# Moving layer 0's step products from GpSimd to VectorE, and layer 1's output projection behind the next image's first states

## The chip, the cores and the metric

The kernel runs on one core of a Trainium2 chip. A core has five engines that run their own instruction streams and meet at semaphores: TensorE (PE, matrix products into PSUM), VectorE (DVE), ScalarE (ACT), GpSimd (POOL) and SyncE (SP, which issues the DMAs here). The metric is the device time of one execution in microseconds (us), lower is better. PSUM is the memory into which TensorE writes (`bank` in the code), SBUF the larger one beside it (`room`, `u`, `y`, `pictures` and the rest).

## What is computed

Eight images of 32x32 pixels and 192 channels run through two layers. Cut to what matters, with `_gn` a group norm and `L` = 1024 pixels:

```python
def layer0(x):                        # 384 inner channels, 16 states, 8 scan orders
    xc, z = split(_gn(x) @ W_in.T)    # then a 3x3 depthwise convolution and silu on xc
    for k in range(8):                # rows, columns, mirrored, and each of them backwards
        dts, B, C = split(x_proj[k] @ xs[k])
        delta = softplus(dt_proj[k] @ dts + bias[k])
        h = exp(delta * A) * h + (delta * xs[k]) * B      # a scan over the 1024 pixels, per state
        y[k] = sum_n(h[n] * C[n]) + D[k] * xs[k]
    return layernorm(sum_k y[k]) * silu(z) @ W_out.T
def layer1(x):                        # the same frame, four orders with one set of weights,
    ...                               # and decay * cumsum(source / decay) in place of the scan
    return layernorm(y) * silu(z) @ W_out
x = x + layer0(x); x = x + layer1(x)
```

## The kernel before

The images are worked through one after the other; for each, layer 0's scans, layer 0's tail, layer 1's front, layer 1's scans and layer 1's tail. The tail of layer 1 also holds the front of the next image's layer 0 (input projection, convolution, first projections). Every engine has its whole order written out by hand, as a function per stage (`scans0`, `tail0`, `front1`, `scans1`, `tail1`); an engine takes its own instructions strictly in that order, and semaphores tie the orders together.

Layer 0's scans run over 384 units per image: `UNITS` counts g over 8 scan orders i, 3 channel tiles j of 128 channels and 16 states n. The 16 units of one (i, j) are called a pass here, so an image has 24 passes. Tiles are 128 partitions x 1024 pixels in float32. For one unit:

- POOL multiplies the pass's step product `du0` (delta times the input, one tile per pass, two buffers) with a row of B that a DMA has spread over the partitions: `source` (L1186). It may run up to 5 units ahead of the scans (`SOURCES`), and waits then for `scan(g - 5)`.
- ACT makes exp(delta * A) into PSUM: `decay` (L930), two buffers, waiting for `scan(g - 2)`.
- DVE does the scan (`scan`, L1355), decay from PSUM and source from SBUF.
- The state is weighted with C and summed over n by PE, in one of three ways. For 9 of 16 states ("by vector") PE spreads the row of C into two PSUM banks called `WORK` (`spread_c`, L584) and DVE multiplies (`weigh`, L1363). For 3 to 5 states ("by pool": n of 2, 6, 10, for tile 0 also 12, sometimes 8) POOL multiplies with a spread row, three units behind its own sources (`POOL_LAG`, L1195). The others ("by turn": 4, 8, 14, and 12 for tiles 1 and 2) PE transposes into `WORK` (L605), ACT scales (L949).

DVE's order is scan 0, scan 1, weighing 0, scan 2, weighing 1 and so on: the weighing of unit g - 1 behind the scan of unit g. `WORK` is the only room for the spread rows, for the turned states and for the "pieces" (projections for coming passes, L454, L556, L566), so each of these waits until the one before has been taken out.

The step product of the next pass is made by POOL behind its source 6 (`du`, L1176), as two instructions of 512 elements per partition: even lines of pixels, and odd lines backwards. For passes 0 to 11 lines are rows of the picture; for passes 12 to 23 they are columns, and `u` is read with a stride. The first pass's product stands at the head of `scans0`.

Layer 1's output projection (`tail1`, L792) is 12 matrix products (24 matmuls in the trace) of two halves c of the output channels by three tiles j by two halves of pixels. It stands on PE behind `head0` of the next image, that is, behind the first projections, and ahead of the first `spread_c`; its first half goes to the banks `YACC`, its second to `WORK`. ACT takes both out (`take_out1`, L1093) in its units 1 and 2, DVE adds them to the image (`residual`, L1495) behind scan 3 into `pictures`. Scan 4 waits for that, since the buffer `o2` lies in the states' room.

Of the kernel before, what the change touches and what calls it, by code (L numbers as in the profile page):

```python
# [6 lines left out]
ALU = mybir.AluOpType  # L7
# [27 lines left out]
LAST_SUM, FIRST_TERM = 2, 4  # L35

# [120 lines left out]

def mm(step):

    return "mm0" if step in AHEAD else "mm"  # L160


def ev(step):

    return "ev0" if step in AHEAD else "ev"
# [20 lines left out]
def program(nc, counts, images, x, out, w_in, conv_w, conv_b, w_x0, w_dt0, dt_b0, a_log0, d0,  # L186
# [3 lines left out]
    with ctx:  # L190
# [77 lines left out]
        o2 = room[0:CH, 18:20, :]  # L268
# [3 lines left out]
        def whole(lo):  # L272
# [10 lines left out]
                 "xz", "shift", "silu", "mm", "ev", "mm0", "ev0", "stat0", "stat1", "gs0", "gs1", "xn", "pad", "conv", "u",  # L283
                 "p1", "p2", "parts", "dl", "du",
# [25 lines left out]
        def _(sp):  # L310
# [51 lines left out]
            def rows0(b):  # L362
                store_bc(b, 0, 0)
                for g, (i, j, n) in enumerate(UNITS):
# [6 lines left out]
                    if by_pool(i, j, n):  # L371
                        c = POOLED.index((i, j, n))
                        if c == CROWS - 1 and b > 0:

                            sp.wait_ge(S["mm"], at("mm", ("out", 1, 1), b - 1))
# [63 lines left out]
        def _(pe):  # L439
# [170 lines left out]
            def begin_sums(b, i, j):  # L610
                if i * J + j > 0:
                    pe.wait_ge(S["y_turned"], at("y_turned", i * J + j - 1, b))
                elif b > 0:
                    pe.wait_ge(S["ev"], at("ev", ("out", 1, 0), b - 1))
# [46 lines left out]
            def scans0(b):  # L661
                for g in range(len(UNITS) + LAST_SUM + 1):
# [22 lines left out]
                    if n == FIRST_TERM:  # L685
                        begin_sums(b, i, j)
# [67 lines left out]

            def tail1(b):
# [29 lines left out]
                pe.wait_ge(S["load_wout1"], at("load_wout1", 0, b))  # L785
                for c, banks in ((0, (YACC, YACC + 1)), (1, WORK)):
                    if c == 1:
                        wait_free(0, 1)
                    for j in range(J):
                        pe.wait_ge(S["gat"], at("gat", (1, j), b))  # L790
                        for h in range(2):
                            ins = nc.tensor.matmul(bank[0:CH, banks[h], :], wout[1][:, j, c * CH:(c + 1) * CH],  # L792
                                                   y[:, j, halves(h)], start=(j == 0), stop=(j == J - 1))
                    ins.then_inc(S["mm"], note("mm", ("out", 1, c)))
                free[0] = free[1] = ("ev", ("out", 1, 1), b)
# [15 lines left out]
        def _(act):  # L811
# [157 lines left out]
            def scans0(b):  # L969
                for g in range(len(UNITS) + 2):  # L970
# [8 lines left out]
                    if g in (1, 2) and b > 0:  # L979
                        take_out1(b - 1, g - 1)  # L980
# [110 lines left out]
            def take_pair(b, step, dst, banks, rows=P, func=ACT.Copy, **kw):  # L1091
                act.wait_ge(S["mm"], at("mm", step, b))
                nc.scalar.activation(dst, bank[0:rows, banks[0]:banks[1] + 1, :].rearrange("p h t -> p (h t)"),  # L1093
                                     func, **kw).then_inc(S["ev"], note("ev", step))
# [20 lines left out]
            def take_out1(b, c):  # L1115
                take_pair(b, ("out", 1, c), o2[:, c, :], ((YACC, YACC + 1), WORK)[c], rows=CH)

            def tail0(b):
# [4 lines left out]
                for c, banks in ((0, WORK), (1, SPARE)):  # L1123
                    take_pair(b, ("out", 0, c), o2[:, c, :], banks, rows=CH)
# [41 lines left out]
        def _(pool):  # L1166
            def du(b, l, i, j):
                if l == 1:
                    pool.wait_ge(S["dl"], at("dl", (1, 0, j), b))
                    pool.wait_ge(S["yinit"], at("yinit", (1, j), b))  # L1170
                    nc.gpsimd.tensor_tensor(u[:, j, :], delta1[:, j, :], u[:, j, :], ALU.mult).then_inc(
                        S["du"], note("du", (1, 0, j)))
                    return
                pool.wait_ge(S["dl"], at("dl", (0, i, j), b))
                for d, dt, src in zip(stored(du0[:, (i * J + j) % 2, :]), stored(delta0[:, j, :]), lines(u[:, j, :], SCANS[i][1])):
                    nc.gpsimd.tensor_tensor(d, dt, src, ALU.mult).then_inc(S["du"], note("du", (0, i, j)))  # L1176
# [21 lines left out]
            def scans0(b):  # L1198
                du(b, 0, 0, 0)
                for g in range(len(UNITS)):  # L1200
                    source(b, g)
                    i, j, n = UNITS[g]
                    if g >= POOL_LAG and by_pool(*UNITS[g - POOL_LAG]):
                        weigh(b, g - POOL_LAG)
                    ahead = i * J + j + 1
                    if n == 6 and ahead < PASSES:
# [413 lines left out]
```

## Time and profile before

| | us |
|---|---|
| median of 3 runs (15345.07 to 15356.31) | 15351.98 |
| the profiled execution, its own time | 15355.73 |
| its span, first to last instruction | 15353.9 |
| DVE busy in the span (91%) | 13974.8 |
| POOL busy (89%) | 13679.9 |
| PE busy (78%) | 11962.6 |
| ACT busy (67%) | 10343.2 |

All eight images look alike. Of some 1912 us for one, layer 0's scans take 1183, layer 0's tail and layer 1's front some 100, layer 1's scans some 566 and the tail of layer 1 the rest. In a timeline a row is a start, a duration, engine, line, operation, what it writes and reads, and how many like instructions were drawn together; in brackets is the idle time of the engine before it and what ended that. Instructions of an engine overlap by some 0.06 to 0.09 us, so starts lie a little closer than durations say.

### The profile page before, as it was taken

The page shows a single profiled execution, that of the slowest core. Times are in us where ns is not written, and L with a number is a line of the kernel's source. Part 1 is how long each engine was busy: PE and PEld are TensorE (multiplying, and loading weights), DVE is VectorE, ACT ScalarE, POOL GpSimd, SP SyncE. Part 2 cuts the span into 40 slices and gives each one's busy share as a digit, 9 for nine tenths or more (in the row PEclk, how much of TensorE's full clock was granted, in tenths as well). Part 3 has the DMA queues.
Part 4 walks back from the last instruction along what each step waited for, and adds up shares of the span by engine and source line. Part 5 has one row for each costly group of instructions (what it writes and reads, how often), then busy time and mean ns, then how long its engine had stood idle before and what let it go on. Part 6 is the DMA issues. An engine that isn't in the chain of part 4 may idle for free.

```text
span 15353.9 us, 137291 instructions
## 1 busy us (share of the span) xinstructions
PE 11962.6 (78%) x45056; PEld 6538.9 (43%) x45056; DVE 13974.8 (91%) x8019; ACT 10343.2 (67%) x14003; POOL 13679.9 (89%) x5828
## 2 busy tenths in 40 slices
PE   6777877778777787777877778777787777877778
PEld 4543345433444334443345433444334443345433
DVE  8998989989899899998999989999898998989988
ACT  5666766667666676666766667666676666766667
POOL 7997989979899798997889978899789997899978
PEclk8898988989889898898988989889898898988989
DMA  5662256622566225662256622666226662266622
GB/s 188 213 214 95 88 188 215 213 93 85 193 214 215 90 82 196 215 215 86 82 201 213 216 85 80 204 215 214 84 77 209 215 214 81 77 212 214 213 76 76
DMA packets 687758, 2440.08 MB, mean 159 GB/s; under 512 B 78268, under 2 KB 100040, under 8 KB 687048
## 3 DMA queue, kind: packets, MB, share of 16 engines
q1 hardware_dynamic: 687048, 2431.29, 46.6%
q8 instruction: 362, 5.93, 0.2%
q14 instruction: 348, 2.85, 0.1%
HBM read 2415.26 MB, written 15.73 MB: 158 GB/s over the span
## 4 chain that ended last, share of the span: by engine, by line
POOL 48%; issue 18%; DMA 11%; DVE 10%; PE 10%; ACT 3%; POOLq 0%; DVEq 0%; SPq 0%; ACTq 0%
POOL room L1186 26%; DMA room<-bc_rows 11%; POOL room L1229 7%; POOL room L1195 4%; POOL room L1232 4%; POOL room L1221 4%; DVE room L1420 4%; PE bank L720 3%; POOL room L1176 2%; PE bank L454 2%; DVE room L1355 2%; DVE u L1312 1%; DVE room L1440 1%; DVE room L1429 1%; PE bank L792 1%
## 5 line engine op out<-in xcount | busy, mean ns | idle before, releaser
L1355 DVE TENSOR_TENSOR_SCAN room<-bank,room 128x1024 f32<-128x1024 f32 x3072 | 6903.6, 2275 | 327.5 <-issue 170.2
L1186 POOL TENSOR_TENSOR room<-room 128x1024 f32<-128x1024 f32 x3072 | 7168.0, 2374 | 0.6
L930 ACT ACTIVATE bank<-room,a 128x1024 f32<-128x1024 f32 x3072 | 3429.7, 1127 | 1046.0 <-DVE room L1355 1031.7
L720 PE MATMUL bank<-room,identity 128*128 128x512 f32 x6144 | 3007.4, 640 | 855.5 <-DVE room L1440 733.2
L1420 DVE TENSOR_TENSOR_SCAN room<-bank,room 128x1024 f32<-128x1024 f32 x1536 | 3430.9, 2273 | 54.1 <-POOL room L1229 32.4
L632 PE MATMUL bank<-identity,room 128*128 128x128 f32 x19456 | 2818.1, 295 | 4.3 <-DVE room L1363 4.1
L632 PEld LDWEIGHTS bank<-identity,room 128*128 128x128 f32 x19456 | 2525.1, 154 | 524.6 <-issue 315.6
L1363 DVE TENSOR_TENSOR room<-room,bank 128x1024 f32<-128x1024 f32 x1728 | 2071.7, 1199 | 406.1 <-PE bank L584 403.0
L720 PEld LDWEIGHTS bank<-room,identity 128*128 128x128 f32 x6144 | 1200.5, 203 | 2663.4 <-issue 1270.3
L1229 POOL TENSOR_TENSOR room<-room 128x1024 f32<-128x1024 f32 x768 | 2225.5, 2921 | 56.2 <-ACT room L1051 26.7
L584 PE MATMUL bank<-parts,pick_row 96*128 96x512 bf16 x3456 | 1245.9, 421 | 718.2 <-DVE room L1363 451.4
L1195 POOL TENSOR_TENSOR room<-room 128x1024 f32<-128x1024 f32 x704 | 1671.6, 2374 | 120.9 <-DVE room L1355 120.0
L949 ACT ACTIVATE room<-bank,c_turned 128x128 f32<-128x128 f32 x5120 | 1391.1, 382 | 541.7 <-PE bank L605 541.7
L605 PE MATMUL bank<-identity,room 128*128 128x128 f32 x5120 | 798.9, 307 | 982.5 <-DVE room L1363 981.7
L1051 ACT ACTIVATE room<-room,a 128x1024 f32<-128x1024 f32 x1248 | 1365.8, 1138 | 4.5
L626 PE MATMUL bank<-room,identity 128*128 128x512 f32 x2560 | 1323.1, 642 | 4.1 <-DVE room L1363 4.1
L1232 POOL TENSOR_TENSOR room<-room 128x1024 f32<-128x1024 f32 x480 | 1160.9, 2428 | 0.0
L605 PEld LDWEIGHTS bank<-identity,room 128*128 128x128 f32 x5120 | 642.4, 158 | 1167.4 <-DVE room L1363 1164.2
L1176 POOL TENSOR_TENSOR room<-room,u 128x512 f32<-128x512 f32 x384 | 545.8, 1449 | 572.1 <-ACT room L913 572.1
L1221 POOL TENSOR_TENSOR room<-u,room 128x1024 f32<-128x1024 f32 x384 | 971.3, 2529 | 7.8 <-DMA room<-bc_rows 7.8
L584 PEld LDWEIGHTS bank<-parts,pick_row 96*128 96x128 bf16 x3456 | 326.4, 102 | 1475.5 <-DVE room L1363 599.5
L814 ACT ACTIVATE room<-bank 128x512 f32<-128x512 f32 x544 | 324.7, 598 | 752.3 <-PE bank L556 348.7
(133 smaller groups left out, 11560.2 us busy)
## 6 DMA issues: line engine op xcount, KB each, us to landing
room<-bc_rows SPq DMA_DIRECT2D x4544, 512.0 KB, 4.6
wx<-in_w_x SPq DMA_DIRECT2D x65, 162.0 KB
bc_rows<-xdbl SPq DMA_DIRECT2D x72, 128.0 KB, 4.7
pictures<-in_x SPq DMA_DIRECT2D x8, 768.0 KB, 9.0
out_x<-pictures SPq DMA_DIRECT2D x8, 768.0 KB, 7.7
weights<-in_w_in SPq DMA_DIRECT2D x16, 288.0 KB, 6.7
room<-in_w_in SPq DMA_DIRECT2D x16, 288.0 KB, 5.8
room<-in_w_out SPq DMA_DIRECT2D x16, 288.0 KB, 6.2
```

The source lines that it names most:

```text
L584: ins = nc.tensor.matmul(bank[:, WORK[h], :], pick_row[:, N + n:N + n + 1].broadcast_to([XR, P]), parts[:, i % 2, halves(h)], start=True, ...
L632: ins = nc.tensor.matmul(whole(YACC)[:, k * P:(k + 1) * P], state0[:, g % STATES, k * P:(k + 1) * P], identity[:, :], start=(first_of_layo ...
L720: ins = nc.tensor.matmul(dst, identity[:, :], rhs, start=(q == 0), stop=(q == Q - 1))
L930: nc.scalar.activation(whole(DECAY0[g % 2]), delta0[:, j, :], ACT.Exp, scale=a0[:, col:col + 1]).then_inc(S["decay"], note("decay", (i, j, ...
L1186: nc.gpsimd.tensor_tensor(source0[:, g % SOURCES, :], du0[:, (i * J + j) % 2, :], b_ring0[:, g % BROWS, :], ALU.mult).then_inc(S["source"] ...
L1195: nc.gpsimd.tensor_tensor(state, state, c_ring0[:, c, :], ALU.mult).then_inc(S["weigh_pool"], note("weigh_pool", (i, j, n)))
L1221: nc.gpsimd.tensor_tensor(src, u[:, j, :], b_ring1[:, m % BROWS1, :], ALU.mult).then_inc(S["source1"], note("source1", (j, n)))
L1229: nc.gpsimd.tensor_tensor(state, state, src.rearrange("p (r c) -> p c r", r=SIDE), ALU.mult).then_inc(S["gated"], note("gated", (j, n, q)))
L1232: nc.gpsimd.tensor_tensor(state, state, src, ALU.mult).then_inc(S["gated"], note("gated", (j, n, q)))
L1355: nc.vector.tensor_tensor_scan(run(state0[:, g % STATES, :]), run(whole(DECAY0[g % 2])), run(source0[:, g % SOURCES, :]), 0.0, ALU.mult, A ...
L1363: nc.vector.tensor_tensor(state, state, whole(WORK[0]), ALU.mult).then_inc(S["weigh"], note("weigh", UNITS[g]))
L1420: nc.vector.tensor_tensor_scan(state, dec, state, 0.0, ALU.mult, ALU.add).then_inc(S["scan1"], note("scan1", (j, n, q)))
```

## The change

Layer 0's step products move from POOL to DVE, in halves: for pass 0 both at the head of `scans0`, for the later ones the first half behind scan 5 and the second behind scan 7 of the pass before. They have the semaphore `du` to themselves now; layer 1's products stay on POOL with a semaphore of their own, `du1`.

Layer 1's output projection, except for the last image, leaves `tail1` and comes in four pieces behind the spreads of the next image's units 0, 1, 3 and 4 (in unit 4 behind the turning of a state): four matrix products, two, four, two. Both halves go through `YACC`; the second waits until ACT has taken the first. ACT takes them in its units 4 and 6 (before: 1 and 2), DVE adds them behind scans 5 and 9 (before: both behind scan 3). `o2` gets a place of its own for layer 1, so scan 4 waits for nothing more. The first pass's sums begin one unit later (5 for 4). For the last image the two halves of the projection now follow each other through `YACC`.

```diff
+OUT1 = {0: (0, (0, 1)), 1: (0, (2,)), 3: (1, (0, 1)), 4: (1, (2,))}
...
-        o2 = room[0:CH, 18:20, :]
+        o2 = [room[0:CH, 18:20, :], room[0:CH, 7:9, :]]
...
 PE, scans0:
-                    if n == FIRST_TERM:
+                    if b > 0 and g in OUT1:
+                        out1(b - 1, *OUT1[g])
+                    if n == FIRST_TERM and i * J + j > 0 or g == FIRST_TERM + 1:
                         begin_sums(b, i, j)
...
+            def out1(b, c, tiles):
+                if c == 1 and 0 in tiles:
+                    pe.wait_ge(S["ev1"], at("ev1", ("out", 1, 0), b))
...
+                for j in tiles:
+                    pe.wait_ge(S["gat"], at("gat", (1, j), b))
+                    for h in range(2):
+                        ins = nc.tensor.matmul(bank[0:CH, YACC + h, :], wout[1][:, j, c * CH:(c + 1) * CH],
+                                               y[:, j, halves(h)], start=(j == 0), stop=(j == J - 1))
...
 ACT, scans0:
-                    if g in (1, 2) and b > 0:
-                        take_out1(b - 1, g - 1)
+                    if g in (4, 6) and b > 0:
+                        take_out1(b - 1, int(g == 6))
...
 POOL:
-                for d, dt, src in zip(stored(du0[:, (i * J + j) % 2, :]), stored(delta0[:, j, :]), lines(u[:, j, :], SCANS[i][1])):
-                    nc.gpsimd.tensor_tensor(d, dt, src, ALU.mult).then_inc(S["du"], note("du", (0, i, j)))
...
-                    if n == 6 and ahead < PASSES:
-                        du(b, 0, ahead // J, ahead % J)
...
 DVE:
+            def du(b, pass_, part):
+                i, j = pass_ // J, pass_ % J
+                dve.wait_ge(S["dl"], at("dl", (0, i, j), b))
+                nc.vector.tensor_tensor(stored(du0[:, pass_ % 2, :])[part], stored(delta0[:, j, :])[part],
+                                        lines(u[:, j, :], SCANS[i][1])[part], ALU.mult).then_inc(
+                    S["du"], note("du", (0, i, j)))
...
-                if g == 4 and b > 0:
-                    dve.wait_ge(S["res"], at("res", (1, 1), b - 1))
...
-                    if g == 3 and b > 0:
-                        residual(b - 1, 1, 0)
-                        residual(b - 1, 1, 1)
+                    if g in (5, 9) and b > 0:
+                        residual(b - 1, 1, int(g == 9))
+                    if g < len(UNITS) and n in (5, 7) and i * J + j + 1 < PASSES:
+                        du(b, i * J + j + 1, int(n == 7))
```

How the rows stand now: on PE at the second image's first units, before (L792 is the projection, L584 a spread of C, L556 a piece for pass 2, L605 a turning, L632 a sum):

```order
L575 MATMUL bank<-parts,minus_two 32x512
L792 MATMUL bank<-y,room 96x512 x12
L584 MATMUL bank<-parts,pick_row 128x512 x4
L556 MATMUL bank<-xdbl,weights 128x512 x2
L605 MATMUL bank<-identity,room 128x128 x8
```

and after (L772, L591, L563, L612, L639 are the same five):

```order
L582 MATMUL bank<-parts,minus_two 32x512
L591 MATMUL bank<-parts,pick_row 128x512 x2
L772 MATMUL bank<-y,room 96x512 x4
L772 MATMUL bank<-y,room 96x512 x2
L563 MATMUL bank<-xdbl,weights 128x512 x2
L612 MATMUL bank<-identity,room 128x128 x8
L639 MATMUL bank<-identity,room 128x128 x16
```

The projection has gone from one block ahead of the first spread to two pieces behind spreads 0 and 1 (shown) and two more behind spread 3 and the turning of state 4.

On DVE behind the last product of layer 1's tail (L1490), in the second image, before (L1355 is a scan, L1363 a weighing, L1495 the sum with the image):

```order
L1490 TENSOR_TENSOR y<-y,room 128x1024 x3
L1355 SCALAR_TENSOR_TENSOR room<-bank,room 128x1024 x2
L1363 TENSOR_TENSOR room<-room,bank 128x1024
L1355 SCALAR_TENSOR_TENSOR room<-bank,room 128x1024
L1495 TENSOR_TENSOR pictures<-pictures,room 96x1024 x2
```

and after (L1346 is a half of a step product, L1364 a scan, L1372 a weighing, L1508 the sum with the image; first the head, then from scan 5 on):

```order
L1502 TENSOR_TENSOR y<-y,room 128x1024 x3
L1346 TENSOR_TENSOR room<-room,u 128x16x32 x2
L1364 SCALAR_TENSOR_TENSOR room<-bank,room 128x1024 x2
...
L1508 TENSOR_TENSOR pictures<-pictures,room 96x1024
L1346 TENSOR_TENSOR room<-room,u 128x16x32
L1364 SCALAR_TENSOR_TENSOR room<-bank,room 128x1024
L1372 TENSOR_TENSOR room<-room,bank 128x1024
```

Two halves now stand ahead of the first scan, and one each behind scans 5 and 7 in every pass but the last.

## Rows read from the trace of the kernel before

**Rows 1.** Groups by line, 1977 to 3165 us: busy, mean ns, idle before.

```profile
L1355 DVE TENSOR_TENSOR_SCAN room<-bank,room 128x1024 f32<-128x1024 f32 x384 | 862.9, 2275 | 37.6 <-issue 19.8 <-POOL room L1186 8.6 <-ACT bank L930 5.8
L1363 DVE TENSOR_TENSOR room<-room,bank 128x1024 f32<-128x1024 f32 x216 | 258.9, 1199 | 53.8 <-PE bank L584 53.5
...
L1186 POOL TENSOR_TENSOR room<-room 128x1024 f32<-128x1024 f32 x384 | 897.1, 2383 | 0.1
L1195 POOL TENSOR_TENSOR room<-room 128x1024 f32<-128x1024 f32 x88 | 209.8, 2384 | 17.1 <-DVE room L1355 16.9
L1176 POOL TENSOR_TENSOR room<-room,u 128x512 f32<-128x512 f32 x48 | 68.6, 1461 | 70.8 <-ACT room L913 70.8
```

**Rows 2.** Busy time by stretch: length, then PE, PEld, DVE, ACT, POOL.

```profile
82.00:1253.00 1171.00, 901.51 (x4372) 578.06 (x4371) 1094.74 (x603) 768.17 (x1272) 1154.03 (x517) 0.89 0.62 213
1982.00:3165.00 1183.00, 913.29 (x4397) 581.73 (x4396) 1099.10 (x605) 770.31 (x1275) 1156.44 (x518) 0.89 0.63 212
```

**Rows 3.** Waits, 1977 to 3165 us: total, times, longest.

```profile
DVE room L1363 <- PE bank L584: 53.5, 32, 16.2
...
DVE room L1355 <- issue: 19.8, 21, 1.4
...
DVE room L1355 <- POOL room L1186: 8.6, 3, 7.8
```

**Rows 4.** Timeline of POOL: step products of rows and of columns, and sources.

```profile
2062.59 2.48 POOL L1176 TENSOR_TENSOR room<-room,u 128x512 f32<-128x512 f32 x2
...
2085.90 18.56 POOL L1186 TENSOR_TENSOR room<-room 128x1024 f32<-128x1024 f32 x8
...
2645.90 3.02 POOL L1176 TENSOR_TENSOR room<-room,u 128x512 f32<-128x512 f32 x2
```

**Rows 5.** Timelines of DVE and POOL around the sums with the image.

```profile
2009.64 4.85 DVE L1495 TENSOR_TENSOR pictures<-pictures,room 96x1024 f32<-96x1024 f32 x2
...
2008.87 2.35 POOL L1186 TENSOR_TENSOR room<-room 128x1024 f32<-128x1024 f32 x1
2011.16 4.44 POOL L1176 TENSOR_TENSOR room<-room,u 128x512 f32<-128x512 f32 x2
```

**Rows 6.** Groups by line and shape, whole span: DVE with two tensors from SBUF.

```profile
L1403 DVE TENSOR_TENSOR_SCAN room<-one,room 128x1024 f32<-128x1024 f32 x64 | 227.1, 3549 | 0.0
L1403 DVE TENSOR_TENSOR_SCAN room<-bank,room 128x1024 f32<-128x1024 f32 x32 | 70.7, 2271 | 56.1 <-ACT room L918 56.1
L1490 DVE TENSOR_TENSOR y<-y,room 128x1024 f32<-128x1024 f32 x48 | 57.9, 1222 | 11.2 <-ACT y L1112 11.2
```

**Rows 7.** Timelines of POOL, DVE, ACT and PE at the second image's start.

```profile
1977.23 2.48 POOL L1176 TENSOR_TENSOR room<-room,u 128x512 f32<-128x512 f32 x2 [70.78 <-ACT room L913]
2006.56 2.35 POOL L1195 TENSOR_TENSOR room<-room 128x1024 f32<-128x1024 f32 x1 [12.93 <-DVE room L1355]
...
1982.23 4.58 DVE L1355 TENSOR_TENSOR_SCAN room<-bank,room 128x1024 f32<-128x1024 f32 x2 [7.81 <-POOL room L1186]
2002.99 1.22 DVE L1363 TENSOR_TENSOR room<-room,bank 128x1024 f32<-128x1024 f32 x1 [16.18 <-PE bank L584]
...
1988.48 0.59 ACT L897 ACTIVATE parts<-bank 32x512 bf16<-32x512 f32 x1 [1.68 <-PE bank L575]
...
1988.37 12.72 PE L792 MATMUL bank<-y,room 128*96 128x512 f32 x24
2002.29 0.59 PE L584 MATMUL bank<-parts,pick_row 96*128 96x512 bf16 x2 [1.20 <-ACT room L1093]
```

**Rows 8.** Timeline of DVE, states 3 to 7 of pass 13.

```profile
2639.77 4.46 DVE L1355 TENSOR_TENSOR_SCAN room<-bank,room 128x1024 f32<-128x1024 f32 x2
2644.85 1.22 DVE L1363 TENSOR_TENSOR room<-room,bank 128x1024 f32<-128x1024 f32 x1 [0.61 <-PE bank L584]
2646.95 4.47 DVE L1355 TENSOR_TENSOR_SCAN room<-bank,room 128x1024 f32<-128x1024 f32 x2 [0.88 <-ACT bank L930]
...
2660.66 1.22 DVE L1363 TENSOR_TENSOR room<-room,bank 128x1024 f32<-128x1024 f32 x1 [3.66 <-PE bank L584]
```

More of the change, by code:

```diff
@@ L155 @@
     (name, 0, h) for name in ("rest", "last") for h in range(2)}
+LATE = {("out", 1, 0), ("out", 1, 1)}
 def mm(step):
-    return "mm0" if step in AHEAD else "mm"
+    return "mm0" if step in AHEAD else "mm1" if step in LATE else "mm"
 def ev(step):
-    return "ev0" if step in AHEAD else "ev"
+    return "ev0" if step in AHEAD else "ev1" if step in LATE else "ev"
 class Counts:
@@ L753, in tail0 @@
                 free[0] = free[1] = ("ev", ("out", 0, 0), b)
+            def out1(b, c, tiles):
+                if c == 1 and 0 in tiles:
+                    pe.wait_ge(S["ev1"], at("ev1", ("out", 1, 0), b))
+                pe.wait_ge(S["load_wout1"], at("load_wout1", 0, b))
+                for j in tiles:
[3 more added lines that the diff above has]
+                                               y[:, j, halves(h)], start=(j == 0), stop=(j == J - 1))
+                if J - 1 in tiles:
+                    ins.then_inc(S["mm1"], note("mm1", ("out", 1, c)))
             def tail1(b):
@@ L784, in tail1 @@
                     head0(b + 1)
[L785 to L795, printed above, removed]
+                else:
+                    for c in range(2):
+                        out1(b, c, range(J))
             pe.wait_ge(loaded, 16 * LOADS)
@@ L1115, in take_out1 @@
             def take_out1(b, c):
-                take_pair(b, ("out", 1, c), o2[:, c, :], ((YACC, YACC + 1), WORK)[c], rows=CH)
+                take_pair(b, ("out", 1, c), o2[1][:, c, :], (YACC, YACC + 1), rows=CH)
             def tail0(b):
@@ L1123, in tail0 @@
                 for c, banks in ((0, WORK), (1, SPARE)):
-                    take_pair(b, ("out", 0, c), o2[:, c, :], banks, rows=CH)
+                    take_pair(b, ("out", 0, c), o2[0][:, c, :], banks, rows=CH)
             def tail1(b):
@@ L1234, in scans1 @@
                     if n == 12 and j + 1 < J:
-                        du(b, 1, 0, j + 1)
+                        du1(b, j + 1)
             def make_taps():
@@ L1371, in scans0 @@
             def scans0(b):
+                du(b, 0, 0)
+                du(b, 0, 1)
                 for g in range(len(UNITS) + 1):
```

37 lines of the change are left out of this document (16 added, 21 removed).

## The prediction

> **What bounds the kernel now.** I read the groups by line for layer 0's scans of the second image first, with POOL and DVE side by side [rows 1]. The 384 sources, 88 weighings and 48 half products of POOL have next to no idle time among them: 0.1 us before the sources, 17.1 before the weighings, 12.9 of that once at the image's start [rows 7]; the 70.8 before the products is the time outside the stage. In the same stretch of 1183 us DVE is busy for 1099.1 [rows 2]. So POOL sets the pace once an image runs, and DVE has 84 us of slack. The waits then say what DVE's slack is made of [rows 3]: 19.8 us in 21 waits with no releaser shown, each up to 1.4, and 8.6 on sources, of which 7.8 is the first. I read the 21 as waits for POOL's sources too, since POOL shows no pause around them. That is 20.6 us behind the first scan. The rest of the scans' idle time is mostly ACT's [rows 1]. The weighings wait 53.5 us for PE's spread rows, 32 times, 16.2 of it once, at the start, where PE is busy for 12.72 us with the output projection [rows 7]. So the stage is close to balanced: POOL never rests, and DVE is 93% busy. To move work from the one to the other pays only if it costs little on DVE.
>
> **What leaves POOL.** 48 half products an image, 68.6 us [rows 1], and nothing is added there. Sources and weighings remain: 472 instructions at a distance of 2.31 us (eight take 18.56 [rows 4]), 1090 us. POOL stops being the bound, and DVE's 20.6 us of waiting for sources go. DVE is late next.
>
> **What one half costs DVE when nothing is in its way.** A product of 1024 elements from two SBUF tensors takes 1.22 us in layer 1's tail, where POOL rests [rows 6]. Half of that is 0.61, less some 0.08 by which neighbours overlap: 0.53. For columns POOL's pair takes 3.02 us where rows take 2.48 [rows 4], a factor of 1.22, so 0.65. Passes 1 to 11 have 22 halves and passes 12 to 23 have 24: 22 x 0.53 + 24 x 0.65 = 27.3 us an image. The two of pass 0 stand at the head, where they replace POOL's pair and POOL rests.
>
> **What it costs with POOL at work.** This is the disputed price, and the trace has it in two places. The sums with the image also read two SBUF tensors: with POOL running the two together take 4.85 us, against 1.22 for one such operation alone [rows 5, 6], and POOL's pair beside them takes 4.44 instead of 2.48 [rows 4, 5]. The rows interlock: the sum that starts at 2009.64 finds POOL's source (2008.87, 2.35 long) under way, and POOL's own next instruction is stretched. A scan with ones from SBUF takes 3.549 us as a mean of 64, against 2.271 with ones from PSUM [rows 6], 1.28 more. DVE's scans and weighings have one operand in PSUM and show no such stretch. So a DVE operation with two SBUF inputs first waits for the end of POOL's current instruction, and POOL's next one waits for DVE. The Trainium skill says the same: its page SBUF — State Buffer, section Who interferes with whom, states that a VectorE instruction with two SBUF inputs contends with a GpSimd instruction that reads SBUF, and that whoever holds the shared port first holds it for the whole instruction. That rule speaks against this change, and the trace agrees with its 4.85 and 3.549 us.
>
> How long does a half wait? At most the rest of POOL's instruction, between 0 and some 2.2 us. POOL's place is set by its own lag: weighing 2 needs scan 2, and weighing 6 needs scan 6. A scan is 2.19 behind its neighbour (two take 4.46 [rows 8]), a weighing 1.11. From the end of scan 2 DVE needs weighing 1, scans 3 and 4, weighing 3 and scan 5: 8.8 us to the first half. POOL starts weighing 2 there some 0.15 late (scan 2 follows weighing 0, which starts at 2002.99, by 1.1 and ends at 2006.4; POOL starts at 2006.56 [rows 7]) and goes on with sources 6, 7 and 8; the fourth ends at 9.4, so the half waits about 0.5. For tile 1, DVE loses 0.88 more before scan 5 to ACT [rows 8], misses that end and waits for the next, about 1.9. From the end of scan 6 to the second half there are 3.3 us; POOL does weighing 6 and source 10 in that time, until 4.8, so it waits about 1.35. Over the tiles that is (0.5 + 0.5 + 1.9) / 3 = 0.97 and 1.35, a mean of 1.16. The nearest rows say 1.24 and 1.28. I take 1.16: 46 x 1.16 = 53.4 us. The ends are 0 and 2.2, that is 0 and 101 us.
>
> A price from a page alone: VectorE: DVE Perf Modes, in the section on the TRN2 errata, gives 691 ns for such an operation of 512 elements. With that in place of 0.53 to 0.65, less the same overlap, an image would be some 1 us longer, by an estimate.
>
> **What the halves give back.** They stand where DVE often waits for PE: 16 of the 31 later waits for spread rows, 17.1 us, come right before the weighings of states 5 and 7, as the 3.66 in [rows 8], and six waits of 0.5 before scan 7. A half in front gives that chain time, so these 20 go; of the other 20 I let 4 be made up. Together 24 us an image. What I can't exclude is that the chain through PE and ACT only shifts: then it is 0.
>
> **The output projection.** Today weighing 0 starts at 2002.99 because 12.72 us of products stand ahead of spread 0 [rows 7]. ACT's last part of C lands at 1989.07 [rows 7], so spread 0 can follow at once and weighing 0 can start at 1989.9: 13.1 earlier, a wait of 4.3 instead of 16.2. But the pieces still have to be done, now between the spreads: the first, 8 of 24 matmuls or 4.2 us, holds spread 1 until 1995 (2.0 of waiting before weighing 1); spread 3 stands behind the second piece, the delta piece and ACT's first taking (0.7); and the turning of state 4 stands behind the third piece, ACT's second taking behind the fourth, and ACT's scaling of state 4 behind that, so weighing 5 waits some 2.7. Sum 9.7 where 16.2 was: 6.5 won for images 2 to 8. SyncE's wait for the second half comes at C's third row, needed by the weighing of state 10; hidden, since scan 10 is over ten us later. The sums with the image keep their price (4.85); separate places change nothing. The two first halves take 1.2 where POOL's pair took 2.48 [rows 7], and the first scan starts 1.2 earlier. In the last image the second half of the projection waits for the taking of the first: 1 us, once.
>
> **The sum.** Image 2, first scan at 1982.23 to the last weighing's end at 3164.9: 1182.7 = 1099.1 busy + 83.6 idle (37.6 - 7.8 + 53.8 [rows 1]). After: 1099.1 + 27.3 + 53.4 busy or held, and 83.6 - 20.6 - 6.5 - 24 = 32.5 idle, 1212.3. That is 29.6 longer, 28.4 with the earlier start. Seven such images: 199. Image 1: 1171 = 1094.7 busy [rows 2] + 76.3; the same without the 6.5 gives 1207.1, 34.9 longer with the start. With the 1 at the end: 235 us. The profiled execution took 15355.7, 3.7 above the median, so 15,591; I say 15,590. A half breaks even at some 1.12 us, 0.5 of waiting.
>
> **The rivals.**
> 1. *Faster: the halves find POOL at rest.* With less to do POOL is up to five sources ahead; if it has stopped where the halves come, or just ends its instruction there, the waiting falls to nothing. Then 53.4 x 8 = 427 fewer: 15,163. It decides from a mean wait below 0.5. For it: POOL has 1090 us of work in 1212, so it must rest somewhere. Against it: weighing 6 is its resting place, and the way there from weighing 2 is five instructions, 11.6 us, longer than the 8.8 to the first half. Chance of landing faster by over 0.2% (about what a measurement of this kernel can tell from no change): 0.20.
> 2. *Nothing to see: waits near 0.5.* If ACT's 0.88 goes with a slower DVE and the second half comes closer to an end, gain and loss meet: within 31 us, 15,325 to 15,386. Chance 0.12.
> 3. *Worse: the PE waits stay.* Without the 24 us of relief: 192 more, 15,782. The chains are driven by DVE's own weighings, which is for it; against it, the example's 3.66 hangs on PE's queue and not on the moment of DVE's arrival. Whole POOL instructions waited for would give 8 x 46 x 1.04 = 383 more, 15,973. Together 0.13.
> 4. *The head gives nothing*, if the pieces run into the turning of state 4 harder than I count: 7 x 6.5 = 45 more, inside the forecast.
>
> **How the numbers follow.** The forecast, 15,400 to 15,700, has 0.55. Slower by over 0.2% is that and case 3: 0.68; same 0.12; faster 0.20. The range takes in most of the faster case's reach and case 3: 15,200 to 15,800.
>
> **What would show it.** Right: DVE's group of halves with 384 entries and a mean near 1.8 us, the 16 in the head at 0.6; POOL busy some 340 us less in all (546 of products gone, its neighbours stretched by about 0.55 for each of 368 halves), and idle before its weighings; the scans' waits without a releaser gone; the 16.2 at the start down to about 4, with new ones behind it. Wrong: halves with a mean below 1.2, or PE's waits before weighings 5 and 7 as large as before.

## The result: slower, by more than forecast

The changed kernel takes 15757.9 us (median of 4 runs, 15747.93 to 15768.05) where the kernel before takes 15351.15 beside it: 1.0265 times as long, 95% interval 1.0247 to 1.0283. That is 407 us more; the forecast said 235 more, 15,590. The sign and the range held, the size did not. The profiled execution has a span of 15764.2 us.

The page of the changed kernel: busy time of the engines, then the costliest groups of layer 0 (line, engine, operation, tiles, count | busy us, mean ns of one | idle us ahead of them, and what ended most of it).

```profile
PE 12107.0 (77%) x45056; PEld 6633.2 (42%) x45056; DVE 14659.5 (93%) x8403; ACT 10348.4 (66%) x14003; POOL 13367.0 (85%) x5444
...
L1195 POOL TENSOR_TENSOR room<-room 128x1024 f32<-128x1024 f32 x3072 | 7353.2, 2426 | 691.0 <-DVE room L1346 586.0
L1364 DVE TENSOR_TENSOR_SCAN room<-bank,room 128x1024 f32<-128x1024 f32 x3072 | 6908.5, 2272 | 99.8 <-ACT bank L944 39.8
...
L1372 DVE TENSOR_TENSOR room<-room,bank 128x1024 f32<-128x1024 f32 x1728 | 2064.7, 1195 | 321.6 <-PE bank L591 320.2
...
L1204 POOL TENSOR_TENSOR room<-room 128x1024 f32<-128x1024 f32 x704 | 1660.2, 2358 | 711.7 <-DVE room L1364 688.5
...
L1346 DVE TENSOR_TENSOR room<-room,u 128x512 f32<-128x512 f32 x384 | 750.1, 1955 | 29.7 <-ACT room L927 29.7
```

L1195 are POOL's sources, L1364 DVE's scans, L1372 its weighings, L1204 POOL's weighings, and L1346 the new halves. POOL is no longer the bound: ahead of its weighings it rests 711.7 us, and DVE ends that rest. DVE spends 750.1 us on the halves, 1.955 each. The 16 at the images' heads, where POOL rests, are part of that and take 0.688 on average; the other 368 take 2.01.

The second image is the one that the forecast was worked out on. Groups of DVE in that stretch, 2024 to 3264 us, then busy time in a window from its first scan to its last weighing (PE, PEld, DVE, ACT, POOL, then PE's granted clock):

```profile
L1364 DVE TENSOR_TENSOR_SCAN room<-bank,room 128x1024 f32<-128x1024 f32 x384 | 863.6, 2272 | 11.7 <-POOL room L1195 4.9 <-ACT bank L944 3.5 <-issue 2.6
L1372 DVE TENSOR_TENSOR room<-room,bank 128x1024 f32<-128x1024 f32 x216 | 258.1, 1195 | 40.3 <-PE bank L591 40.2
L1346 DVE TENSOR_TENSOR room<-room,u 128x512 f32<-128x512 f32 x48 | 95.9, 2000 | 2.2 <-ACT room L927 2.2
...
L1508 DVE TENSOR_TENSOR pictures<-pictures,room 96x1024 f32<-96x1024 f32 x2 | 2.4, 1194 | 0.0
```

```profile
2029.00:3264.00 1235.00, 928.30 (x4399) 591.86 (x4398) 1184.48 (x651) 772.43 (x1276) 1120.97 (x472) 0.88 0.60 203
```

Against [rows 1] and [rows 2] this gives the ledger of one image, from its first scan to the end of its last weighing:

| us, image 2 | before | forecast | measured |
|---|---|---|---|
| DVE busy (with the halves' waits for the port) | 1099.1 | 1179.8 | 1184.5 |
| scans waiting, without the first | 29.8 | | 9.2 |
| weighings waiting | 53.8 | | 40.3 |
| both waits | 83.6 | 32.5 | 49.5 |
| length | 1182.7 | 1212.3 | 1234.0 |

The seven later images are 51.4 us longer each on average, the first one 50.1: 7 x 51.4 + 50.1 = 410, and the two profiled spans differ by 15764.2 - 15353.9 = 410.3. So all of the time is in this stage. The forecast missed some 22 us per image: 5 of it is work or holding of DVE, 17 are waits: 12 that it expected to vanish, and 5 new ones.

### The profile page after: what moved, and what is told of

It is laid out like the page before. It is cut to its first block, busy times and chain, and to the rows that moved or that the text cites. A ratio compares the mean times of both kernels' runs of the same rounds, so it can differ in the third digit from the quotient of the medians.

```text
span 15764.2 us, 137304 instructions
## 1 busy us (share of the span) xinstructions
PE 12107.0 (77%) x45056; PEld 6633.2 (42%) x45056; DVE 14659.5 (93%) x8403; ACT 10348.4 (66%) x14003; POOL 13367.0 (85%) x5444
## 4 chain that ended last, share of the span: by engine, by line
DVE 28%; PE 25%; POOL 23%; issue 16%; ACT 6%; DMA 3%; DVEq 0%; SPq 0%; POOLq 0%; ACTq 0%
DVE room L1364 12%; POOL room L1195 9%; POOL room L1233 6%; DVE room L1372 6%; PE bank L639 5%; DVE room L1432 4%; PE bank L729 4%; POOL room L1225 4%; POOL room L1236 3%; PE bank L633 3%; PE bank L461 3%; DMA room<-bc_rows 3%; PE bank L591 2%; PE bank L612 2%; DVE u L1316 1%
## 5 line engine op out<-in xcount | busy, mean ns | idle before, releaser
L1195 POOL TENSOR_TENSOR room<-room 128x1024 f32<-128x1024 f32 x3072 | 7353.2, 2426 | 691.0 <-DVE room L1346 586.0
L1364 DVE TENSOR_TENSOR_SCAN room<-bank,room 128x1024 f32<-128x1024 f32 x3072 | 6908.5, 2272 | 99.8 <-ACT bank L944 39.8
L729 PE MATMUL bank<-room,identity 128*128 128x512 f32 x6144 | 3016.7, 642 | 856.8 <-DVE room L1452 725.4
L1432 DVE TENSOR_TENSOR_SCAN room<-bank,room 128x1024 f32<-128x1024 f32 x1536 | 3430.3, 2272 | 53.8 <-POOL room L1233 34.5
L639 PE MATMUL bank<-identity,room 128*128 128x128 f32 x19456 | 2793.6, 293 | 4.3 <-DVE room L1372 4.1
L639 PEld LDWEIGHTS bank<-identity,room 128*128 128x128 f32 x19456 | 2496.8, 153 | 535.5 <-issue 295.8
L1372 DVE TENSOR_TENSOR room<-room,bank 128x1024 f32<-128x1024 f32 x1728 | 2064.7, 1195 | 321.6 <-PE bank L591 320.2
L1233 POOL TENSOR_TENSOR room<-room 128x1024 f32<-128x1024 f32 x768 | 2238.9, 2938 | 58.6 <-ACT room L1065 29.1
L1204 POOL TENSOR_TENSOR room<-room 128x1024 f32<-128x1024 f32 x704 | 1660.2, 2358 | 711.7 <-DVE room L1364 688.5
L591 PE MATMUL bank<-parts,pick_row 96*128 96x512 bf16 x3456 | 1214.1, 414 | 718.4 <-DVE room L1372 434.9
L612 PE MATMUL bank<-identity,room 128*128 128x128 f32 x5120 | 844.7, 319 | 1133.7 <-DVE room L1372 1133.6
L633 PE MATMUL bank<-room,identity 128*128 128x512 f32 x2560 | 1413.9, 681 | 4.1 <-DVE room L1372 4.1
L612 PEld LDWEIGHTS bank<-identity,room 128*128 128x128 f32 x5120 | 678.9, 164 | 1320.0 <-DVE room L1372 1314.2
L1236 POOL TENSOR_TENSOR room<-room 128x1024 f32<-128x1024 f32 x480 | 1152.2, 2410 | 0.0
L591 PEld LDWEIGHTS bank<-parts,pick_row 96*128 96x128 bf16 x3456 | 329.0, 103 | 1452.9 <-DVE room L1372 582.3
L1346 DVE TENSOR_TENSOR room<-room,u 128x512 f32<-128x512 f32 x384 | 750.1, 1955 | 29.7 <-ACT room L927 29.7
```

The costliest lines, as they stand in the source:

```text
L591: ins = nc.tensor.matmul(bank[:, WORK[h], :], pick_row[:, N + n:N + n + 1].broadcast_to([XR, P]), parts[:, i % 2, halves(h)], start=True, ...
L612: ins = nc.tensor.matmul(whole(WORK[0])[:, cut], state0[:, g % STATES, cut], identity[:, :], start=True, stop=True, is_transpose=True)
L633: ins = nc.tensor.matmul(bank[:, YACC + h, :], identity[:, :], state_turned[:, slot, halves(h)], start=False, stop=False)
L639: ins = nc.tensor.matmul(whole(YACC)[:, k * P:(k + 1) * P], state0[:, g % STATES, k * P:(k + 1) * P], identity[:, :], start=(first_of_layo ...
L729: ins = nc.tensor.matmul(dst, identity[:, :], rhs, start=(q == 0), stop=(q == Q - 1))
L1195: nc.gpsimd.tensor_tensor(source0[:, g % SOURCES, :], du0[:, (i * J + j) % 2, :], b_ring0[:, g % BROWS, :], ALU.mult).then_inc(S["source"] ...
```

## Where the miss lies: two places in the trace

**Weighing 9.** I added up the weighings' waits for spread rows by state, over the 24 passes of an image, as a mean of the eight images:

| us per image | before | after |
|---|---|---|
| weighings 5 and 7, and scan 7 | 24.0 | 4.6 |
| weighing 9 | 6.6 | 22.6 |
| weighings 11 and 13 | 5.4 | 1.9 |
| scans 10, 12 and 14 | 17.4 | 2.0 |

The relief in front of weighings 5 and 7 came, and two states later 16.0 of it were gone again. Here is one of these places, pass 16 of the second image: DVE first, then PE, then windows of PE's work before the idle time and of its chain behind it (the clock is the figure ahead of the last two).

```profile
2881.84 2.49 DVE L1346 TENSOR_TENSOR room<-room,u 128x512 f32<-128x512 f32 x1
2884.25 2.28 DVE L1364 TENSOR_TENSOR_SCAN room<-bank,room 128x1024 f32<-128x1024 f32 x1
2886.45 1.20 DVE L1372 TENSOR_TENSOR room<-room,bank 128x1024 f32<-128x1024 f32 x1
2887.56 4.46 DVE L1364 TENSOR_TENSOR_SCAN room<-bank,room 128x1024 f32<-128x1024 f32 x2
2893.78 1.22 DVE L1372 TENSOR_TENSOR room<-room,bank 128x1024 f32<-128x1024 f32 x1 [1.75 <-PE bank L591]
```

```profile
2887.79 1.94 PE L612 MATMUL bank<-identity,room 128*128 128x128 f32 x8 [2.65 <-DVE room L1372]
2889.53 3.62 PE L633 MATMUL bank<-room,identity 128*128 128x512 f32 x4
2892.94 0.73 PE L591 MATMUL bank<-parts,pick_row 96*128 96x512 bf16 x2
```

```profile
2880.00:2882.90 2.90, 2.90 (x14) 1.52 (x15) 2.90 (x2) 1.66 (x3) 2.90 (x2) 1.00 0.43 153
2883.00:2885.10 2.10, 2.10 (x10) 1.55 (x8) 2.10 (x2) 0.45 (x1) 2.10 (x2) 0.50 0.17 68
2885.00:2893.00 8.00, 5.35 (x14) 2.99 (x14) 7.03 (x4) 5.12 (x11) 7.02 (x4) 0.50 0.56 205
```

Weighing 7 ends at 2887.65 and frees `WORK`. Only then can PE turn state 8 (L612), sum (L633) and spread row 9 (L591), and DVE has just two scans, 4.46 us, to fill that time. PE's granted clock is 0.50 here (the lower of its two levels), and the turn takes 1.94 us and the sum 3.62. PE had idled 2.65 us behind the second half, but that isn't what lowered the clock: it was 1.00 up to 2882.9 and 0.50 from 2883.0 on, with PE busy without a pause in both windows, and the idle time began only at 2885.1. The same pass in the kernel before, PE:

```profile
2802.15 1.06 PE L605 MATMUL bank<-identity,room 128*128 128x128 f32 x8 [1.21 <-DVE room L1363]
2803.05 1.88 PE L626 MATMUL bank<-room,identity 128*128 128x512 f32 x4
2804.77 0.75 PE L584 MATMUL bank<-parts,pick_row 96*128 96x512 bf16 x2
```

There PE idled 1.21 us, the turn took 1.06 and the sum 1.88. Besides, scan 10 of that pass waited 1.0 us in the kernel before, and spread 9 was ready behind it. Without that wait weighing 9 would have come at 2806.41, still behind the end of spread 9 at 2805.52, so in this pass it is the slower work of PE that makes the new wait. In general a scan's wait ahead of a weighing covers PE's chain, but of the scans in the table only scan 10 stands between weighings 7 and 9, and its waits were 3.7 us per image (now 0), so the lost cover is at most about a quarter of the 16.0. By passes the 16.0 are 6.7 in passes 13 to 21, 6.0 in passes 10 to 12, 1.6 in passes 22 and 23 and 1.6 in the first ten.

**Step 13 at the image's start.** DVE and POOL, then SyncE's queue (SPq: L366 spreads a row of B or C over the partitions, L428 stores the finished picture):

```profile
2072.91 1.19 DVE L1508 TENSOR_TENSOR pictures<-pictures,room 96x1024 f32<-96x1024 f32 x1
...
2084.23 2.29 DVE L1364 TENSOR_TENSOR_SCAN room<-bank,room 128x1024 f32<-128x1024 f32 x1 [1.32 <-issue]
2088.86 2.29 DVE L1364 TENSOR_TENSOR_SCAN room<-bank,room 128x1024 f32<-128x1024 f32 x1 [2.33 <-POOL room L1195]
```

```profile
2081.80 2.35 POOL L1195 TENSOR_TENSOR room<-room 128x1024 f32<-128x1024 f32 x1 [12.12 <-DVE room L1364]
```

```profile
2074.14 0.34 SPq L428 DMA_DIRECT2D out_x<-pictures  x1
2074.52 9.97 SPq L366 DMA_DIRECT2D room<-bc_rows  x5
```

The change puts the second sum with the image behind scan 9 (2072.91). SyncE's store of that picture stands in its queue ahead of the row of B for step 13, and waits for the sum; the row leaves at 2074.52 and POOL's source 13 starts at 2081.80, after 12.12 us of rest. The row of the trace names a scan as what ended that rest, but that scan is no part of it: the DMA behind the store is. Scans 13, 14 and 16 wait 1.32, 2.33 and 1.33 us for it, 5.0 in this image.

## The experiments

The verdicts compare each kernel with runs of the kernel before on the same chip: 15350.7 us for the first four, 15347.1 for the last three.

**Each part alone.** `e1_du_only` is the kernel before with the step products on DVE, and the projection in one piece as it was:

```diff
-                    if n == 6 and ahead < PASSES:
-                        du(b, 0, ahead // J, ahead % J)
...
+                    if g < len(UNITS) and n in (5, 7) and i * J + j + 1 < PASSES:
+                        du(b, i * J + j + 1, int(n == 7))
```

> The kernel before with one part of the change: layer 0's step products on VectorE in halves behind scans 5 and 7; the output projection stays one block ahead of the first spreads. Theory (the price is the wait for GpSimd's running instruction, 46 halves an image at some 2.0 us, and PE's waits only shift): nearly the whole loss is here, 15,700 to 15,790 us; the start of an image keeps its wait of 16 us, and the third B row of the store's queue is not late. Rival (the two parts of the change hurt each other, the projection's pieces and the halves meeting at the start): the halves alone cost half of it or less, below 15,600.

It takes 15769.5 us, 1.0274 times as long (1.0258 to 1.0289). So the step products alone cost 419 us, all of the loss, as expected. The waits of scans 10, 12 and 14, 17.4 us per image before, are 0 in this run. `e2_out_only` is the other part alone, with the products left on POOL:

```diff
-                    if g in (1, 2) and b > 0:
-                        take_out1(b - 1, g - 1)
+                    if g in (4, 6) and b > 0:
+                        take_out1(b - 1, int(g == 6))
...
-                        residual(b - 1, 1, 0)
-                        residual(b - 1, 1, 1)
+                    if g in (5, 9) and b > 0:
+                        residual(b - 1, 1, int(g == 9))
```

> The kernel before with the other part alone: the output projection in four pieces behind the first spreads, sums with the image behind scans 5 and 9; the step products stay on GpSimd. Theory: GpSimd sets the pace, and its wait of 12.9 us at an image's start goes, but two new ones come, some 3 us for a B row and up to 12 for the row that SyncE can only fetch when the store of the image is issued, which now waits for the sum behind scan 9. So next to nothing remains: 15,290 to 15,370. Rival (the freed head counts in full): 7 x 13 = 91 us, 15,260.

It takes 15351.95 us, ratio 1.0001 (0.9992 to 1.001): nothing, as expected. But POOL's sources, which in the kernel before had hardly any idle time inside the stage, now wait 91.8 us for DMAs, all of it ahead of source 13: 13.6 in the second image. The other wait that was expected, some 3 us for a row of B, did not show. The page:

```profile
L1200 POOL TENSOR_TENSOR room<-room 128x1024 f32<-128x1024 f32 x3072 | 7182.4, 2386 | 92.4 <-DMA room<-bc_rows 91.8
```

**What the halves wait for.** In `e3_du_psum` the halves of passes 1 to 23 read their first factor from PSUM: the decay of the coming step, which is there anyway, in place of the step size in SBUF. Their number, length, place and access to `u` stay.

```diff
...
+                first = delta0[:, j, :]
+                if g is not None:
+                    dve.wait_ge(S["decay"], at("decay", UNITS[g + 1], b))
+                    first = whole(DECAY0[(g + 1) % 2])
-                nc.vector.tensor_tensor(stored(du0[:, pass_ % 2, :])[part], stored(delta0[:, j, :])[part],
+                nc.vector.tensor_tensor(stored(du0[:, pass_ % 2, :])[part], stored(first)[part],
...
-                        du(b, i * J + j + 1, int(n == 7))
+                        du(b, i * J + j + 1, int(n == 7), g)
```

> The changed kernel, but the halves of passes 1 to 23 multiply the input with the next unit's decay out of PSUM in place of delta out of SBUF (so the step products are other numbers; the instruction, its place, its size and its output stay). One SBUF input is left. Theory (the wait is for the port that GpSimd reads through): halves take 0.7 us for rows and 1.0 for columns, GpSimd's sources are no longer stretched, and most of the 420 us of waiting comes back, part of it as waits for PE: 15,350 to 15,500. Rival (VectorE is simply full, and a half of this shape takes 2 us by itself): within 50 us of the changed kernel, 15,710 to 15,800.

It takes 15303.97 us, ratio 0.9969 (0.9957 to 0.9982), 46 us below the range that was expected: the waits for PE did not grow, as the theory had it, but fell (288.5 us ahead of the weighings instead of 321.6). Groups by shape:

```profile
L1350 DVE TENSOR_TENSOR room<-bank,u 128x512 f32<-128x512 f32 x368 | 315.0, 856 | 0.0
```

The halves take 0.856 us instead of 2.01; POOL's sources shrink to 2.366 from 2.426. That one operand is worth 15757.9 - 15304.0 = 454 us, more than the whole loss, and 368 halves that are shorter by 1.15 make 424 of them. The rival, that VectorE is simply full and a half of this shape takes 2 us by itself, falls: with one SBUF input per half the same order beats the kernel before. The run also gives the halves' own price without the wait: 0.666 us on average for rows (0.664 to 0.680), but 1.03 for columns (1.00 to 1.07).

**Another place.** `e4_du_6_10` puts the halves directly behind scans 6 and 10, where POOL was expected to have stopped for DVE:

```diff
+                    if g < len(UNITS) and n in (6, 10) and i * J + j + 1 < PASSES:
+                        du(b, i * J + j + 1, int(n == 10))
                     if g > 0 and by_vector(*UNITS[g - 1]):
                         weigh(b, g - 1)
...
-                    if g < len(UNITS) and n in (5, 7) and i * J + j + 1 < PASSES:
-                        du(b, i * J + j + 1, int(n == 7))
```

> The changed kernel with the halves elsewhere: directly behind scan 6 and scan 10, ahead of the weighing that follows. There GpSimd has just waited for that scan. Theory: the half is issued before GpSimd's weighing has been released, takes the port at once and costs its own 0.7 (rows) or 1.0 us (columns); PE's waits before weighings 5 and 9 shrink by as much, those before 7 come back: 15,330 to 15,450. Rival (the place doesn't matter, a half costs half a GpSimd instruction on average wherever it stands): a mean near 2 us and 15,700 to 15,800.

15670.8 us, ratio 1.0207 (1.0192 to 1.0222): between theory and rival. The page:

```profile
L1372 DVE TENSOR_TENSOR room<-room,bank 128x1024 f32<-128x1024 f32 x1728 | 2076.8, 1202 | 377.9 <-PE bank L591 373.8
...
L1204 POOL TENSOR_TENSOR room<-room 128x1024 f32<-128x1024 f32 x704 | 1852.2, 2631 | 503.6 <-DVE room L1364 502.0
```

The halves shrink to 1.58 us on average, 159 us in all. Only 80 of the 368 find POOL at rest, as the theory wanted for all. Against that the weighings wait 56 us longer for PE (377.9 against 321.6), and POOL's weighings are stretched from 2.358 to 2.631 us. And 14 halves take over 2.9 us; 12 of these take 8.4 to 10.7 us. The longest of the second image, DVE and then POOL:

```profile
2094.05 10.68 DVE L1346 TENSOR_TENSOR room<-room,u 128x512 f32<-128x512 f32 x1
```

```profile
2088.01 9.29 POOL L1195 TENSOR_TENSOR room<-room 128x1024 f32<-128x1024 f32 x4
2097.26 2.33 POOL L1204 TENSOR_TENSOR room<-room 128x1024 f32<-128x1024 f32 x1
2099.56 4.63 POOL L1195 TENSOR_TENSOR room<-room 128x1024 f32<-128x1024 f32 x2
2108.15 2.34 POOL L1195 TENSOR_TENSOR room<-room 128x1024 f32<-128x1024 f32 x1 [3.96 <-DVE room L1364]
```

DVE comes at 2094.05. POOL passes from one instruction to the next four times without giving way, until it has nothing left to do at 2104.19; the half ends at 2104.73. The other eleven long ones go the same way, past three or four such changes, up to a rest of POOL.

**The store.** `e5_store_late` is the changed kernel with SyncE's store six steps later:

```diff
-                    if g == 12 and b > 0:
+                    if g == 18 and b > 0:
```

> The changed kernel with one number altered: SyncE issues the previous image's store of the finished sums in the eighteenth step of the next image instead of the twelfth, so that the row of B for step 13 no longer stands behind a wait for VectorE's residual. Theory (the store stands ahead of the row in SyncE's queue): GpSimd's 12.1 us wait ahead of the source of step 13 goes, and with it the 5.0 us per image that scans 13, 14 and 16 wait, so 7 x 5.0 = 35 us: 15,705 to 15,735 us. Rival (GpSimd is only late elsewhere, VectorE's time comes back as port waits or waits for TensorE): 15,745 to 15,770 us.

15714.07 us, ratio 1.0239 (1.0223 to 1.0254), 44 us less than the changed kernel (40 when each is taken against its own runs of the kernel before: 367 us against 407); its runs, 15701 to 15720, all lie below that kernel's 15748 to 15768. POOL's idle time ahead of its sources falls from 691.0 to 606.3 us, which is little more than the 585.9 outside the stage:

```profile
L1195 POOL TENSOR_TENSOR room<-room 128x1024 f32<-128x1024 f32 x3072 | 7353.4, 2427 | 606.3 <-DVE room L1346 585.9
```

The theory holds; the missed queue cost 5.0 us per image by the waits and 5.7 to 6.3 by the time (40 / 7 and 44 / 7). Part of it lay in the halves, which fall from 750.1 to 736.0 us. The four longest of the changed kernel, 4.64 to 5.97 us, all stand in the pass behind the late row; here, and in `e1_du_only`, where the row isn't late either, none is longer than 2.97. Most likely the late row leaves POOL with work in hand that it goes through without giving way.

**The clock.** `e6_pe_zeros` is the changed kernel with two more matmuls per pass, ahead of step 8, that add zeros to the sums while PE would idle (`zero` is a column of zeros, set once):

```diff
+                    if g < len(UNITS) and n == 8:
+                        for h in range(2):
+                            nc.tensor.matmul(bank[:, YACC + h, :], identity[:, :], zero[:, :].broadcast_to([P, HT]),
+                                             start=False, stop=False)
```

> The changed kernel with two more TensorE matmuls in every pass, ahead of step 8: each adds identity times zeros, 512 columns, to a bank of sums, so the result stays. They lie where TensorE now waits for scan 8 behind the second half (2.65 us of idle in one pass read, after which the granted clock was 0.50 and the eight transposes of step 8 took 1.94 us instead of the 1.06 us that they took in the kernel before). Theory (the wait of weighing 9, 22.6 us per image against 6.6 us before, comes largely from TensorE's work of step 8 running at the lower clock after that idle time): the turn of step 8 takes 1.06 to 1.2 us in passes 13 to 21 instead of a mean of 1.42, the waits of weighing 9 fall by 8 to 14 us per image, and the time is 15,640 to 15,700 us. Rival (those waits come from where the half stands, not from the clock; the added matmuls lengthen TensorE's chain): waits of weighing 9 as now or longer, 15,750 to 15,840 us.

15749.32 us, ratio 1.0264 (1.025 to 1.0278): the same time as the changed kernel. The page:

```profile
L1377 DVE TENSOR_TENSOR room<-room,bank 128x1024 f32<-128x1024 f32 x1728 | 2067.1, 1196 | 292.7 <-PE bank L592 290.1
...
L1351 DVE TENSOR_TENSOR room<-room,u 128x512 f32<-128x512 f32 x384 | 776.2, 2023 | 28.7 <-ACT room L932 28.7
```

The mechanism shows: in passes 13 to 21 the turn of state 8 takes 1.14 us on average instead of 1.44 (put at 1.42 above), and the waits of weighing 9 fall from 22.6 to 17.2 us per image, less than the 8 to 14 expected. But the weighings' waits fall by 28.9 us in all (321.6 to 292.7), while the halves grow by 26.1 (750.1 to 776.2): what is saved in front of a weighing is paid at the halves. I read this as DVE coming to them at another moment of POOL's row of instructions; that is not shown further. So the slower work of PE takes part in the shift to weighing 9, but the total does not hang on it, and my expectation on the time was wrong. `e3_du_psum` divides the shift further: its order is that of the changed kernel and scan 10 waits for nothing there either, but its halves are short, and weighing 9 waits 11.4 us per image. So 4.8 of the 16.0 come without long halves, and 11.2 only with them. How the long halves work on it, beyond the 5.4 that the two matmuls took away, stays open.

**A version that beats both.** `e7_out_only_late` is `e2_out_only` with the store at 18 as in `e5_store_late`.

> The projection in four pieces alone (du on GpSimd in whole passes as in the kernel before), with the store of the sums issued in the eighteenth step of the next image instead of the twelfth. Theory: the pieces give 6 to 8 us per image at the head, and the late row of B behind the store took it back by holding GpSimd 13.6 us per image ahead of the source of step 13; without that the kernel is faster than the one before, 15,250 to 15,310 us. Rival (GpSimd's wait at step 13 was hidden, or another wait takes its place): 15,335 to 15,365 us, as the pieces alone gave.

15307.41 us, ratio 0.9975 (0.9965 to 0.9984): 40 us less than the kernel before, within what was expected. The page:

```profile
L1200 POOL TENSOR_TENSOR room<-room 128x1024 f32<-128x1024 f32 x3072 | 7166.2, 2369 | 0.6
```

POOL's waits for the late row are gone, and what the head gives is left: 40 / 7 = 5.7 us per image, where the forecast had 6.5.

## Right and wrong, step by step

- **What bounds the kernel, and the sign: right.** POOL set the pace; without the products it rests (711.7 us ahead of its weighings), and DVE gets a price that is higher than what it saves. The 19.8 us of scans without a releaser [rows 3] fell to 2.6: they had been waits for POOL, since the waits of scans 10, 12 and 14 are 0 in `e1_du_only` and stay in `e2_out_only` (18.5 us per image). The signs that were named came near: halves of 1.955 us for 1.8, 0.688 in the head for 0.6, and POOL busy 313 us less for 340.
- **The waits for the port: right.** Forecast 53.4 us per image. In image 2 the 46 halves take 94.6 us; less their own 22 x 0.666 and 24 x 1.03 (from `e3_du_psum`) that leaves 55.2. The first halves were to wait 0.97 and the second 1.35; less the same prices they waited 1.15 and 1.37 us for rows and 0.69 and 1.42 for columns, as means of the eight images. The longer wait of the first half fell where it was forecast, on the passes of tile 1: for rows 1.86 us, where 1.9 was forecast, against 0.85 and 0.59 in tiles 0 and 2. That the agreement is so close is partly luck: four of the halves in tile 1 took 4.64 to 5.97 us, which the hand count had no place for (without them it is 1.50), and the first halves of columns waited less than forecast.
- **The price of a half itself: mis-sized for columns.** The factor of 1.22 was POOL's [rows 4]. DVE's is 1.03 / 0.666 = 1.55: some 0.3 us more on 24 halves, 7 us per image. For rows 0.666 less the overlap is 0.59, where halving a longer operation had given 0.53: 1 us per image. The Trainium skill has a note on its page SBUF — State Buffer, in the section Door 1: The DMA port swizzle, that accesses which cross to a new 16-byte line pay a penalty. The columns of `u` step by 128 bytes, and the runs' 1.03 against 0.666 goes the same way; the note gives no price.
- **The sums with the image: a small miss on the good side.** "Separate places change nothing" was wrong: each now takes 1.19 us where the pair took 4.85 [rows 5], since POOL rests beside both. That is 2.5 us per image.
- **The 24 us of relief: wrong, and the largest miss.** It came where it was put (24.0 to 4.6 in front of weighings 5 and 7 and scan 7), and 16.0 came back in front of weighing 9. In image 2 the waits outside the head and the new ones of step 13 fell by 11.2 instead of 24. The step that failed is the choice against the third rival's mechanism, "the chain through PE and ACT only shifts": that what goes at one state comes back at another. It is shown, but only for about half of the 24 us, and the waits before weighings 5 and 7 did not stay, as that rival's title had it. The rival was named at 15,782, and the measured time lies 24 us from it and 168 from the forecast; that it lies so close is luck, since the price of the columns and the late row, which the rival did not have, make up the rest of the miss.
- **The head: right in itself, and a queue missed.** The waits there were forecast at 9.7 where 16.2 had been; ahead of weighings 0, 1 and 5 they are 4.71, 2.99 and 1.18, together 8.9. But "SyncE's wait ... hidden" looked only at the row of C. The store of the picture, which waits for the later sum, stands in the same queue ahead of a row of B: 5 us of scans' waits per image, 40 to 44 us in all by `e5_store_late`, and the whole gain of the pieces in `e2_out_only`. There the fourth rival, a head that gives nothing, is what came, by a cause that it did not name.
- **Together:** per image 10 more for the halves, less 2.5 for the sums with the image and 3 for neighbours that run a little shorter, and 13 plus 5 less 1 (the head) of waits, give the 22 us by which the image is longer than forecast.
- **Rival 1, halves that find POOL at rest, falls:** of the 176 halves of rows in passes 1 to 11 two take less than 0.8 us, and no half of columns takes less than 1.42. Its condition was well put, though: where the wait is taken away the kernel is faster than before (0.9969).

## What to carry to other kernels

- Before moving an elementwise operation from GpSimd to VectorE, look at its operands. With two in SBUF and GpSimd busy it costs two to three times its own length here (1.93 against 0.67 us for rows, 2.09 against 1.03 for columns); with one of them read in PSUM, that surcharge went.
- Waits of engines that run in step can cover each other. A wait that is taken away at one state is only won if the chain that the same weighing drives has slack at the next; so sum by place, and ask at each what is late next, two states on as well.
- Of a step that is moved, follow the store that waits for it, and everything that stands behind that store in the same queue.

## What the runs showed of the hardware

- **A waiting DVE can lose to POOL more than once.** The forecast took it that a half waits for the end of POOL's current instruction. Most do (waits of 0.6 and 1.46 us are typical for rows), but some lose at one or more changes of POOL's instruction and wait until POOL runs out of work: four halves in the changed kernel, of up to 5.97 us, and twelve in `e4_du_6_10`, of up to 10.7, with three or four changes in between. What decides between the two was not found. The Trainium skill says on its page SBUF — State Buffer, in the section SBUF: two separate sides, that whichever starts first gets the shared ports for the whole instruction; the runs agree that it is held by instruction, and add that the one that waits is not always next.
- **Reading with a step of 128 bytes costs DVE time:** 512 elements with the other operand in PSUM take 1.00 to 1.07 us instead of 0.666 (`e3_du_psum`).
- **PE's granted clock fell while PE was busy, not in the idle time that followed:** in pass 16 it goes from 1.00 to 0.50 some 3 us into a stretch without a pause and 2.1 us before the idle time of 2.65 us; behind that the turn of step 8 takes 1.94 us instead of 1.06. The idle time just ahead of a turn does not tell its clock: in pass 17 it is 3.1 us on average and the turn takes 1.17, in pass 16 it is 2.2 and the turn takes 1.94.
